# Gated cross-attention with an FP6 feed-forward on one core: the columns of c, xn and the dequantised values by DMA and 32x32 blocks instead of TensorE

## What is computed

```python
a = layernorm(x)                                   # (32, 256, 512)
q = a @ w_q.T + b_q;  k = c @ w_k.T + b_k;  v = c @ w_v.T + b_v
s = q k^T / sqrt(32), causal;  p = softmax(s)
x = x + tanh(g_xattn) * ((p v) @ w_o.T + b_o)
y = layernorm(x)
# y and w_f each in blocks of 32: scale = max|block| / 7.5, values rounded to the FP6 grid (steps of 1/8 near 0), times the scale
x = x + tanh(g_ffn) * (dequantised(y) @ dequantised(w_f).T + b_f)
```

## Time and profile before

| | us |
|---|---|
| median of 3 runs | 1426.22 |
| the profiled execution | 1426.4 |
| its span | 1424.4 |

### The profile page before, as it was taken

The page is one execution under the profiler, slowest core; times in us unless marked ns, Lnnn a source line. Parts: engine busy times, 40 slices in busy tenths (PEclk is TensorE's granted clock), DMA queues, the critical chain, the costliest instruction groups (busy, mean ns, idle before and its releaser), DMA issues.

```text
span 1424.4 us, 35124 instructions
## 1 busy us (share of the span) xinstructions
PE 1381.7 (97%) x10844; PEld 1220.1 (86%) x10844; DVE 1102.1 (77%) x4219; ACT 894.7 (63%) x2969; POOL 854.3 (60%) x1387
## 2 busy tenths in 40 slices
PE   6899999999999999999999999999999999999976
PEld 6788888888888888888888888888888888888865
DVE  5778787887788878778788778788778887877763
ACT  4566666666666666666666666666666666666651
POOL 2455665566665666666656566556666566666662
PEclk9999999999999999999999999999999999999988
DMA  8444434444434444434444443444443444443310
GB/s 255 107 112 106 117 93 120 115 128 107 119 90 118 118 125 118 108 94 116 118 119 124 108 114 97 116 117 128 107 119 93 115 117 125 118 111 90 86 51 29
DMA packets 156103, 159.10 MB, mean 112 GB/s; under 512 B 28176, under 2 KB 130576, under 8 KB 155920
## 3 DMA queue, kind: packets, MB, share of 16 engines
q1 hardware_dynamic: 155920, 156.87, 41.6%
HBM read 39.33 MB, written 16.78 MB: 39 GB/s over the span
## 4 chain that ended last, share of the span: by engine, by line
PE 91%; DVE 3%; SPq 2%; issue 1%; ACT 1%; POOL 1%; DMA 1%; DVEq 0%; ACTq 0%; POOLq 0%
PE proj L483 20%; PE proj L484 20%; PE proj L485 20%; PE pT_ps L533 12%; PE oT_ps L550 6%; PE proj L577 6%; PE s_ps L522 4%; PE s_ps L523 2%; SPq L342 1%; DMA all_probs<-in_L_xattn_w_v 1%; ACT all_probs L660 1%; DVE all_probs L807 0%; DMA q_stack<-q_hi 0%; POOL x L448 0%; POOL x L444 0%
## 5 line engine op out<-in xcount | busy, mean ns | idle before, releaser
L410 POOL TENSOR_TENSOR all_probs<-all_probs,rden 128x128 f32<-128x128 f32 (+1 forms) x1024 | 505.0, 514 | 473.3 <-DVE rden L867 472.1
L660 ACT ACTIVATE all_probs<-all_probs,neg_max 128x128 f32<-128x128 f32 (+1 forms) x1024 | 458.7, 451 | 396.7 <-DVE neg_max L807 396.5
L807 DVE CUSTOM_DVE_ANT_0 all_probs<-s_ps,causal 128x128 f32<-128x128 f32 (+1 forms) x1024 | 321.7, 351 | 164.4 <-PE s_ps L523 160.8
L533 PE MATMUL pT_ps<-ident,all_probs 128*128 128x128 f32 x1536 | 264.5, 282 | 6.6 <-POOL all_probs L410 4.3
L660 ACT ACTIVATION_READ_ACCUMULATOR all_probs<-all_probs,neg_max 128x1 f32 x1024 | 195.5, 191 | 0.0
L919 DVE COPY all_probs<-pT_ps 128x384 f32<-128x384 f32 x256 | 139.0, 543 | 66.5 <-PE pT_ps L533 66.5
L533 PEld LDWEIGHTS pT_ps<-ident,all_probs 128*128 128x128 f32 x1536 | 160.4, 142 | 21.7 <-issue 12.7
L522 PE MATMUL s_ps<-k_stack,q_stack 96*128 96x256 f32 x512 | 154.8, 302 | 2.8 <-DVE neg_max L807 2.2
L483 PE MATMUL proj<-cT_hi,wk_hi 128*128 128x256 f32 x512 | 153.2, 299 | 1.9 <-DVE cT_lo L861 1.1
L483 PE MATMUL proj<-aT_hi,wq_hi 128*128 128x256 f32 x512 | 148.0, 289 | 0.4 <-ACT vs L675 0.4
L484 PE MATMUL proj<-cT_lo,wk_hi 128*128 128x256 f32 x512 | 142.4, 278 | 0.0
(11 more groups left out here) (125 smaller groups left out, 3487.3 us busy)
## 6 DMA issues: line engine op xcount, KB each, us to landing
k_stack<-k_hi SPq DMA_DIRECT2D x512, 64.0 KB, 2.0
q_stack<-q_hi SPq DMA_DIRECT2D x512, 64.0 KB, 2.1
xs<-in_x SPq DMA_DIRECT2D x32, 512.0 KB, 4.2
cs<-in_ctx SPq DMA_DIRECT2D x32, 512.0 KB, 6.1
k_stack<-k_lo SPq DMA_DIRECT2D x256, 64.0 KB, 2.0
q_stack<-q_lo SPq DMA_DIRECT2D x256, 64.0 KB, 2.1
out<-x SPq DMA_DIRECT2D x32, 512.0 KB, 3.0
vs<-in_L_xattn_w_k SPq DMA_DIRECT2D x2, 512.0 KB, 7.0
```

Source lines behind the costliest of these rows:

```text
L410: last = nc.gpsimd.tensor_tensor(p, p, rden[:, sd, t, h:h + 1].to_broadcast([P, (1 + t) * P]), ALU.mult)
L533: last = nc.tensor.transpose(pT_ps[h % 2][:, m * P:(m + 1) * P], probs[:, h % P_RING, m * P:(m + 1) * P], ident[:, :])
L660: last = nc.scalar.activation(probs[:, h % P_RING, cols], probs[:, h % P_RING, cols], ACT.Exp, scale=-1.0, bias=neg_max[:, sd, t, h:h + 1] ...
L807: last = nc.vector.tensor_tensor_reduce(probs[:, h % P_RING, cols], s_ps[h % 2][:, cols], causal[:, (1 - t) * P:], 1.0, MASKED, ALU.add, A ...
```

## The change

PE's turning of c, xn and the dequantised values is removed (L577 and the banks for it). Instead:

- `quads_in`: four DMAs bring rows from DRAM into an SBUF tile so that quadrant g (32 partitions) holds features 128 g to 128 g + 127 of 32 tokens on its partitions, in pieces of 512 bytes. c comes so directly. The normalised x, and each half of the dequantised values, are first written to a DRAM tensor of the kernel's own and read back so.
- `turn`: one VectorE transpose of 32x32 blocks per 128 tokens reads such a tile (every fourth element) and writes the columns to one of three places of `cols`; the feature order that comes out is matched by turning the weights of k, q, v and f with every fourth column.
- the upper parts are still ScalarE's, now from SBUF; the lower parts of c and x are VectorE's, now of two SBUF inputs, and those of the dequantised values GpSimd's (`leave`).
- both normalisations are made by ScalarE (`normalised`), with GpSimd computing the shift besides the power, per 128 tokens.
- q and k share one tile `qk` and one tile `stack`; one DMA of 128 KB moves q's and k's part together, so 12 per half and 24 in a step.
- x is read a second time for the residual; `xs` holds one batch.
- `reciprocals` and `divide` take two heads at once, `p` has 6 places instead of 4, and the probabilities are turned in pairs every second slot.
- weights are loaded by ScalarE's queue and SyncE's in pieces of 256 KB, turned in the three `proj` banks over steps 0 to 2, and the quantising of w_f is cut into four.
- the order of all that is set by new tables (`UNITS`, `SLOT_PARTS`, `AT`).

```diff
-UNITS = [("cT", 0, 1), ("cT", 1, 1), ("q", 1, 2), ("dT", 0, 4), ("k", 0, 1), ("dT", 1, 4), ("f", 0, 4), ("xT", 0, 1),
-         ("f", 1, 4), ("xT", 1, 1), ("o", 0, 3), ("o", 1, 3), ("q", 0, 1), ("v", 0, 1), ("k", 1, 1), ("v", 1, 1)]
-SLOT_PARTS = (2, 4, 4, 1, 1, 5, 4, 2, 3, 4, 4, 1, 3, 3, 3, 2)
+UNITS = [("k", 1, 2), ("q", 1, 2), ("f", 0, 4), ("o", 0, 3), ("k", 0, 1), ("q", 0, 1), ("o", 1, 3), ("f", 1, 4),
+         ("v", 0, 1), ("v", 1, 1)]
+SLOT_PARTS = (3, 3, 2, 1, 3, 3, 3, 2, 3, 3, 3, 1, 2, 3, 3, 2)
+AT = {
...
+    "dT": ((4, 0), (4, 6)), "dT_hi": ((4, 1), (4, 7)), "dT_lo": ((4, 1), (4, 7)),
+}
@@ sync
+            def quads_in(dst, rows, signal):
+                for g in range(NQ):
+                    sp.dma_start(dst[g * QUAD:(g + 1) * QUAD, :, :],
+                                 rows[:, g * P:(g + 1) * P].rearrange("(n l) d -> l n d", l=QUAD)).then_inc(signal, 16)
+            def stack_pair(b, half):
+                sp.wait_ge(left["k"], 2 * b + half + 1)
+                sp.wait_ge(left["q"], 2 * b + half + 1)
...
+                for j in range(GROUP):
...
+                    for r, (q_at, k_at) in enumerate(((0, 2), (1, 2), (0, 3))):
+                        sp.dma_start(stack[r * DK:(r + 1) * DK, :, at:at + 2, :].bitcast(F32),
+                                     qk[its, q_at:k_at + 1:k_at - q_at].bitcast(F32)).then_inc(stacked[half][j], 16)
+            def rows_of_d(b, t):
+                sp.wait_ge(xd_ok, 2 * b + t + 1)
+                sp.dma_start(d_dram[b % 2, t * P:(t + 1) * P, :], yz[:, t, :]).then_inc(d_out[t], 16)
+            def quads_of_d(b, t):
+                sp.wait_ge(d_out[t], 16 * (b + 1))
...
+                quads_in(d_quads[:, t * NQ:(t + 1) * NQ, :], d_dram[b % 2, t * P:(t + 1) * P, :], dq_in[t])
@@ gpsimd
-                pool.wait_ge(rden_ok, HEADS * b + h + 1)
+                pool.wait_ge(rden_ok, HEADS * b + h + 2)
...
-                    p = probs[:, h % P_RING, cols]
+                    p = probs[:, at:at + 2, cols]
@@ tensor
-                if kind in ("xT", "cT", "dT"):
...
-                    for c in range(KC):
-                        last = nc.tensor.transpose(bank[:, c * P:(c + 1) * P], src[:, half, c * P:(c + 1) * P],
-                                                   ident[:, :])
@@ vector
+            def turn(kind, b, t, i, quads, arrived, count):
+                dve.wait_ge(arrived, count)
...
+                nc.vector.transpose(columns(kind, t).rearrange("p c (n l) -> p n c l", l=QUAD),
+                                    quads[:, t * NQ:(t + 1) * NQ, :].rearrange("p n (e c) -> p n c e", c=KC)).then_inc(
+                                        turned[kind], 1)
+            def leave(kind, b, t, hi, lo):
...
+                nc.vector.tensor_tensor(lo[:, :, tok], columns(kind, t), hi[:, :, tok].bitcast(F32),
+                                        ALU.subtract).then_inc(lo_ok[kind], 1)
```

More of the change, by code:

```diff
@@ new lines, in ended, with chunks_at, chunks_before, columns @@
+                if at_slot == (slot - 1) % SLOTS and part == PARTS - 1 and live(i - lag):
+                    yield kind, half, i - lag, proj[place_of[kind, 2 * (i - lag) + half] % BANKS]
+        def chunks_at(i, s):
+            for chunk in WEIGHT_TURNS.get((i, s), ()):
+                yield TURNED.index(chunk), *chunk
+        def chunks_before(i, s):
+            return chunks_at(i, s - 1) if s else chunks_at(i - 1, SLOTS - 1)
+        def columns(kind, t):
+            return cols[:, COL_ORDER.index((kind, t)) % COL_PLACES, :, :]
@@ new lines, in weight_bank, with whole, pair_turned, pair_summed @@
+        def weight_bank(u):
+            return proj[place_of["w", u] % BANKS][:, :].rearrange("p (c k) -> p c k", c=KC)
+        def whole(w, rows=KC):
+            return 1 + max(TURNED.index((w, m)) for m in range(rows))
+        def pair_turned(i, s):
+            return i - (2 if s >= PT_LAG else 3), (s - PT_LAG) % SLOTS
+        def pair_summed(i, s):
+            return i - (2 if s >= 2 else 3), (s - 2) % SLOTS
+        def weighed(i, s):
+            for r, slot in enumerate(AV_SLOTS):
+                if s == slot and live(i - 2 - r):
+                    yield i - 2 - r, r
@@ L305, in fused_kernel, with put_out @@
+        def put_out(i, s):
+            for r, slot in enumerate(OUT_SLOTS):
+                if s == slot and live(i - 2 - r):
+                    yield i - 2 - r, r
         block = es.enter_context(nc.Block())
@@ L390, in _ @@
+            for i in range(STEPS):
+                step(i)
             for n in range(2):
-                sp.wait_ge(x1_moved[n], 16 + 16 * (B // 2))
+                sp.wait_ge(x1_out[n], 16 * (B // 2))
         @block.gpsimd
@@ new lines, in unit @@
+                if kind == "k" and b + half:
+                    for j in range(GROUP):
+                        act.wait_ge(stacked[1 - half][j], 3 * 16 * (b + half))
+                at, bias = (0, bias_q) if kind == "q" else (2, bias_k)
+                for m in range(2):
+                    last = nc.scalar.activation(qk[:, at, m, :], bank[:, m * S:(m + 1) * S], ACT.Identity,
+                                                bias=bias[:, 2 * half + m:2 * half + m + 1])
+                last.then_inc(hi_ok[kind], 1)
```

894 lines of the change are left out of this document (464 added, 430 removed), and 4 rows, old and new, of the table WEIGHT_TURNS.

## The result

| | before | after |
|---|---|---|
| median, paired runs | 1427.15 us | 1589.99 us (1588.57 to 1591.02) |
| ratio | | 1.1144, 95% interval 1.1122 to 1.1166 |
| profiled execution, its span | 1426.4, 1424.4 us | 1589.7, 1587.9 us |
| start: to the first weighing of values | 70.23 | 91.65 (+21.4) |
| middle: first to last weighing | 1318.23 | 1449.01 (+130.8) |

The direction was right and the size was not: 1456 was forecast, with 1500 as the upper end. The last three differences are those of the spans, 163.5 us. A step is read off two of TensorE's weighings, 22 steps apart. One of the four paired runs of the kernel before took 6160.5 us; the median holds it by its rank only, and the ratio leaves it out.

A forecast was written before the change was run, and what follows sets the result against it. TensorE bound the kernel before; afterwards a circle of SyncE's DMAs and VectorE's work would, 43.0 us a step against 42.28. 1426.4 plus 22 for 31 steps, 8 for the end, 0 for the start: 1456 us, range 1346 to 1500.

The forecast's parts named there:

- TensorE's 2.71 us a step: TensorE's 768 removed transposes: 86.9 us in all, leaving a step of 39.57 us if TensorE stays the bound.
- Where the waits lie: VectorE's transposes of the values wait for DMA: 4 to 6 us in slot 6, 3 to 5 in slot 0.
- rival 3: VectorE pays for the strided read: 1.3 us a block transpose, 44.9 a step, 1516 us; chance 0.11.
- link 2: VectorE, slots 0 to 3: transposes of values and c, maxima, k, c's lower part, q; 6.3 us.
- link 4: VectorE, slots 6 to 10: transpose, two lower parts, maxima, o, k, moments of x, q; 9.8 us.
- Link 1: SyncE after first-half q is split in slot 10: 12 stackings, store, write of values, reads, landing; 15.2 us.
- link 3: SyncE, before the turn in slot 6: 12 stackings 7.75, reads 1.5, landing 2.4; 11.65 us.
- The larger one holds: Of two circles of waits, 42.97 and 41.7 us, the longer sets the step, taken as 43.0 us.
- second circle: Through TensorE: SyncE's reads, VectorE to slot 8's inverse, `divide`, TensorE slot 10 to q in slot 2, splitting; 41.7 us.
- first circle: SyncE's stackings and values' reads alternating with VectorE's work in slots 0 to 3 and 6 to 10; 42.97 us.
- The start: Kernel's start: w_f's quantising and TensorE's idle time against x through DRAM behind weights' loads; 0 (-10 to +8) us.
- The end: Kernel's end: last values go through DRAM with nothing to cover them; +8 us (5 to 14).

The follow-up runs named there:

- experiment 6: One unused 32-byte tile added to the change: 1578.1 us; to the change with values turned by TensorE again: 1408.9 us; to the kernel before: 1438.2 us.
- experiment 4: The change with 64-row scores: 1554.1 us; with k's lower part stacked in the first batch only, 96 rows: 1517.9; that plus second half's values turned late: 1436.3.

## Why the prediction was wrong in size

- **TensorE's 2.71 us a step: right.** Where nothing else holds, eight of the 24 transposes kept, a step is 40.93 (with the operands in place): 39.57 forecast plus 0.9 for the eight is 40.5. The 0.4 left is about the unexplained 0.002 us per matmul of experiment 6.
- **A circle of SyncE and VectorE takes its place: right, and shown.** Without the values' DMAs in it the same kernel is 171 us faster; moving two turns by one and two slots, with all DMAs kept, removes 95% of the wait.
- **Where the waits lie: right in kind and about in sum.** 4.2 us in slot 6 (4.5 forecast), 2.7 in slot 0 (3 to 5), 213.5 in all (near 250).
- **The circle's length: the failed terms.** The forecast step was 43.0 and the measured one 46.6, which over 31 steps is 112 of the 133 us that were missing. In the step shown the four links are 1.3, 0.55, 0.25 and 1.2 us longer than forecast, 3.3 us together.
- **Links 2 and 4, VectorE.** A transpose was taken at 0.65, the value of a dense pass, by nearness to rows of other operations, though rival 3 stood beside it; it takes 1.10. Three in the circle are 1.35 us: 0.9 in link 2, of which the lower part of c gave back 0.45 (0.75 measured for 1.2), and 0.45 in link 4. The rest of link 4's 1.2 us is many small pieces, none over 0.3 (o with its moments 1.8 for 1.55).
- **Link 1, SyncE: 1.3 us short.** Stackings are 0.64 apart as forecast, but one in each twelve takes 1.2 to 1.3, so that twelve take 8.3 to 8.6 us for 7.7; the store and the landing of the write behind it took 0.6 and 3.6 for 0.43 and 3.2. The same happens in link 3, made up there for the most part by a landing of 2.0 for 2.4.
- **"The larger one holds": right for the change, but the second circle left a path out.** In the change the first circle holds: SyncE's stackings are 29% of the chain of waits, 15 us a step, which is nearly both groups of twelve. The forecast led the second circle over the inverse of slot 8 and `divide` to TensorE's slot 10 and made it 41.7. There is an earlier way into TensorE, and so a longer circle: the lower parts of xn stand behind the waiting turn, q's projection waits for them (84.7 us in 29 waits) and then runs at the lower clock. With a third of the stackings gone it holds the step at 44.4, 3.3 us above what the first circle would have left, and the stackings are 8% of the chain; with the turn moved as well the step falls to 41.4 (experiment 4).
- **The start: failed, 0 (-10 to +8) for +21.4.** The ends of the range were taken from TensorE's idle time, not by following x through its load and xn through DRAM, and what stands behind them. **The end:** +11.3 for +8, inside 5 to 14.
- **Rival 3** priced the stride at 1.3 a transpose and gave 1516; the step it named, 44.9, was nearer than mine, but it too lacked 1.7 us of the middle and the start.

The sum as it should have stood: 31 steps' worth of 4.3 is 133, with 21 and 11: 1592, against 1589.7.

## What to carry to other kernels

When a full engine is relieved by work that goes through DMAs, add up the circle from a buffer's release back to its refill before you add up engines, and ask of each waiting instruction what stands behind it in its program: here two slots of distance between a load and its use were worth 103 us, more than the 86.9 us that the change was meant to save. Move the use, not the load, where the load's place also decides when another buffer comes free. Keep the moved work that has slack (c and xn) and leave what closes the circle (the values) where it was: that version, with its tiles at multiples of 64 bytes, is 1.3% faster than the kernel before (0.9859 to 0.9889).

## What the runs showed of the hardware that was not expected

- A tile's place in SBUF changed TensorE's pace: fp32r matmuls of 256 columns 0.1146 us apart at multiples of 64 bytes and 0.1187 at 32 bytes past one, same program, clock 1.00; 0.8% of this kernel. The columns' tiles moved and the weights' did not; which of the moved tiles counts was not taken apart.
- Scores over 64 rows between matmuls over 128 cost 0.28 us more per head than over 96 rows (0.70 against 0.42 us). The Trainium skill (TensorEngine Tiling (Array Packing), Key Properties) says that a change of tiling mode drains TensorE; the gaps ahead of and behind the 64-row matmuls agree with that, though no run here shows that the mode is what changed.
- Idle time of 2.74 us was followed by 3.7 us at a granted clock of 0.54. The changed kernel has 29 waits of TensorE at this place, 84.7 us in all, and a clock of 0.95 over its middle; in the kernels whose TensorE is full it is 1.00.
- A block transpose of 128 x 512 fp32 takes 0.70 to 0.71 us when it reads densely and 1.10 when it takes every fourth element.
- A VectorE subtraction with two SBUF inputs that starts while a GpSimd instruction is under way ended 0.55 us after that instruction, 1.20 us each in the mean of 62; with GpSimd idle at its start it took 0.67 in the mean (60 of the 64 of xn in the change). The prediction had the rule from one row; new is that a later turn ran into it.
